# Gathers that skip blank rows: a bound on every indirect load and a row number beyond the table

## The chip, the cores and the metric

The kernel runs on one core of a Trainium2 chip. The metric is the device time of one execution in microseconds (us); the numbers of the kernel before are the median of three runs, and one further execution was recorded by the hardware profiler.

## The reference

Four graph layers are applied in turn to 3125 nodes (64 scalars and 32 three-vectors each, 160 words) over 100000 edges. Cut to what matters here:

```python
edge_index = jnp.stack([src, dst])
h = jnp.maximum(_layernorm(x, axis=-1), 0.0)
x = x + _L0_gnn_ref(h, edge_attr_3, edge_attr_64, ..., edge_index)      # gathers rows dst, sums by src
h = jnp.maximum(_layernorm(x, axis=-1), 0.0)
x = x + _L1_gnn_ref(h, node_vec1, src, dst, edge_attr_4, edge_attr_10, ...)  # gathers src, sums by dst
...
# inside each layer
xs = s[dst]                        # one row of the node table for each edge
tp = ...                           # weights from the edge's own features times that row
agg = jax.ops.segment_sum(tp, src, num_segments=N)
```

Layers 1 to 3 gather the row of `src` and sum by `dst`; `dst` comes sorted. Layers 0, 1 and 3 compute the weights of each edge with a small two-layer network; layer 2 has none.

## The kernel before, in words

The edges are put into tiles of 128 (`P`), so that all edges of a tile fall into one bin of 32 nodes. The number of tiles has to be fixed ahead of the data: 880 (`TILES`), in 110 groups (`GROUPS`) of 8 (`GT`). With the inputs of the reference the bins fill 830 tiles in the order of layer 0 and 832 in that of layers 1 to 3 (counted from `src` and `dst`, 32 nodes to a bin, each bin rounded up to whole tiles); the tiles behind them hold only blank rows. For layer 0 the edge rows are scattered to their slots (`scatter`, L697) over a table that was filled with the blank row `blank[0]`, so the unused slots at the end of each bin's last tile are blank too. For layers 1 to 3 a tile is a copy of 128 consecutive rows of the sorted list (`copy_tiles`), whose start is cut off at 100096 rows, behind which `blank[1]` lies; the last rows of a bin's last tile are then rows of the next bin, with a real index, and only the tiles behind the 832nd are blank.

A blank row has key -1, so that the one-hot matrix that sums the tile has a zero column for it and nothing of it reaches a result. Its index (L641) is a row inside the node table: 3 times the slot's place in its group, between 0 and 3069.

A layer is one pass over the 880 tiles. The work is split by engine, and each engine walks through its own loop of groups with semaphores between them:

- SyncE (SP) loads the edge rows of a group into `rows[q]` (two buffers);
- GpSimd (POOL) issues one indirect DMA a tile (L766), eight a group, that gathers 128 rows of 640 bytes from `table_dram[n]` into `gath[q][:, u, :]`. Ahead of tiles 0 and 4 of a group it waits until the consumer has released that half of the buffer of two groups ago (`prod`, or `sc` in layer 2), ahead of tile 0 also for the edge rows;
- ScalarE (ACT) writes the scaled one-hot matrices `sel` (L900) and the hidden layer (L883);
- TensorE (PE) computes the edge weights (L1559) and the sums of a tile (L1578 in layer 2, L1582 and L1584 in the others);
- VectorE (DVE) multiplies weights and gathered rows (L1245, L1249) and adds the sums to the accumulator `acc` (L1233).

Behind the 880th tile of a layer the sums are transposed and multiplied (L1624, L1632), the next layer's table is made and written, POOL clears `acc` meanwhile (L738), and the next layer's gathers start when the table has landed. Ahead of layer 0 POOL scatters 782 times 128 edge rows (L697); then SP loads the first two groups' rows and DVE clears `acc` (L1179).

`gath` has no other writer than the gathers within a layer; between the layers its space is used for `sumT`.

Of the kernel before, what the change touches and what calls it, by code (L numbers as in the profile page):

```python
# [7 lines left out]
I32 = mybir.dt.int32  # L8
# [12 lines left out]
NPAD = BLOCKS * P  # L21
# [4 lines left out]
GT = 8  # L26
FULL_BINS = PAD_NODE // BIN
MAX_TILES = (EDGES + FULL_BINS * (P - 1)) // P + 1
HALF = GT // 2
# [33 lines left out]
PAD_STEP = NODES // (P * GT)  # L63
# [18 lines left out]
def wait(eng, signal, value):  # L82

    if is_static(value) and value <= 0:
        return
    if isinstance(signal, Signal):
        eng.wait_ge(signal.sem, value + signal.base)
    else:
        eng.wait_ge(signal, value)


def pipeline(eng, n, first, last, extra, body):

    for s in range(first):
        body(s, s // 2, s % 2)
    assert (n - first - last) % 2 == 0
    with eng.Fori(0, (n - first - last) // 2) as i:
        for u in range(first, first + 2):
            body(i * 2 + u, i + u // 2, u % 2)
    for s in range(n - last, n + extra):  # L100
        body(s, s // 2, s % 2)
# [109 lines left out]
def gnn_program(nc, t):  # L211

    ctx = ExitStack()
    with ctx:
        def sb(name, shape, dt=F32):
            return ctx.enter_context(nc.sbuf_tensor(name, shape, dt))

        def sem(name):
            return ctx.enter_context(nc.semaphore(name))
# [41 lines left out]
        gath = [sb(f"gath_{q}", [P, GT, NF]) for q in range(2)]  # L261
# [30 lines left out]
        def carve(words):  # L292
            a = used[0]
            used[0] += words
            assert used[0] <= BINS * 256
            return acc[:, a:a + words]
# [20 lines left out]
        base = [carve(COLS) for _ in range(2)]  # L317
# [13 lines left out]
        blank = [carve(GT * w) for w in (A_W, B_W)]  # L331
# [43 lines left out]
        s_scat = [sem(f"s_scat{q}") for q in range(2)]  # L375
        s_copy = [sem("s_copy_sp"), sem("s_copy_act")]
        s_placed = sem("s_placed")
        s_gp = sem("s_gp")
        s_gd = sem("s_gd")

# [86 lines left out]
        def copy_tiles(eng, kind, part, c):  # L467

            for v in range(0, SPREAD // 2, GT):
                u = part * (SPREAD // 2) + v  # L470
                _, start = nc.values_load_multi_w_load_instructions(
                    starts_row[0:1, bass.ds((c - COPY_FROM) * SPREAD + u, GT)], engines=(kind,),
                    min_val=0, max_val=P * COLS, skip_runtime_bounds_check_because="clamped to the number of edges")
                for w in range(GT):
                    eng.dma_start(tiles_b[:, bass.ds((c - COPY_FROM) * (SPREAD // GT) + u // GT, 1), w, :],
                                  given_dram[bass.ds(start[w], P), :].unsqueeze(1)).then_inc(s_copy[part], 16)
# [155 lines left out]
        def _(pool):  # L632
# [5 lines left out]
                pool.memset(blank[o].rearrange("p (t c) -> p t c", t=GT)[:, :, k:k + 1], -1.0).then_inc(s_blank, 1)  # L638
            for o, k in enumerate((A_IDX, B_IDX)):

                pool.iota(blank[o].rearrange("p (t c) -> p t c", t=GT)[:, :, k].bitcast(I32), pattern=[[PAD_STEP, GT]], base=0,  # L641
                          channel_multiplier=PAD_STEP * GT).then_inc(s_blank, 1)
            pool.memset(ident[:, :], 0.0).then_inc(s_cz, 1)
            pool.memset(tri, 1.0).then_inc(s_cz, 1)
# [13 lines left out]
                               pattern=[[-1, P]], channel_multiplier=1)  # L658

            pool.affine_select(out=tri_h, in_=tri_h, compare_op=ALU.is_gt, fill=0.0, base=0,  # L660
                               pattern=[[1, P]], channel_multiplier=-1)
            pool.affine_select(out=tri, in_=tri, compare_op=ALU.is_gt, fill=0.0, base=0,
                               pattern=[[1, P]], channel_multiplier=-1).then_inc(s_const, 1)
# [66 lines left out]
            for n in range(4):  # L730
                L, S = LAYERS[n], s_e[n]
                if n:

                    clear = -(-BINS * L.width // STORES)
                    for i in range(STORES):
                        a, b = clear * i, min(clear * (i + 1), BINS * L.width)
                        wait(pool, s_c[n - 1]["trn"], -(-b // (4 * LAYERS[n - 1].width)))
                        ins = pool.memset(acc[:, a:b], 0.0)  # L738
                    ins.then_inc(S["zero"].sem, 1)
                if n == 1:  # L740
                    wait(pool, s_c[0]["trn"], BLOCKS)
                    pool.memset(acc[:, tail:], 0.0).then_inc(s_lz, 1)

                if n:
                    wait(pool, s_p[n]["td"], 16 * STORES)
                else:
                    for q in range(2):
                        wait(pool, s_p[n][f"td{q}"], 16 * ((BLOCKS + 1 - q) // 2))
                if n:

                    wait(pool, s_e[n - 1]["sc"], TILES)

                def body(g, half, q, n=n, L=L, S=S):

                    wait(pool, S[f"rows{q}"], (half + 1) * (32 if n == 0 else 16))
                    first, w = (GT * 64 + A_IDX - A_SH, A_W - A_SH) if L.rowsA else (B_IDX, B_W)
                    flat = rows[q][:, :, :].rearrange("p t c -> p (t c)")
                    for u in range(GT):
                        if u % HALF == 0:

                            if L.mlp:
                                wait(pool, S["prod"], g * PAIRS + (u + HALF - 2 * GT) // 2)
                            else:
                                wait(pool, S["sc"], g * GT + (u + HALF - 2 * GT))
                            pool.sem_inc(s_apart["pool"], 1)
                        pool.indirect_dma_start(  # L766
                            gath[q][:, u, :], None, table_dram[n][:, :],
                            bass.IndirectOffsetOnAxis(ap=flat[:, u * w + first:u * w + first + 1].bitcast(I32), axis=0)).then_inc(S[f"ga{q}{u // HALF}"].sem, 16)
                pipeline(pool, GROUPS, 2, 0, 0, body)


# [213 lines left out]
        def _(dve):  # L985
# [182 lines left out]
            for n in range(4):  # L1168
# [86 lines left out]
                def edges(g, half, q, n=n, L=L, o=o, select=select, flush=flush, products=products):  # L1255
                    _, bins = nc.values_load_multi_w_load_instructions(  # L1256
                        tile_bins[0:1, bass.ds(g * GT + (LEAD - 2 * L.lag_fl), GT)], engines=(DVE,), min_val=0, max_val=BINS - 1,
                        skip_runtime_bounds_check_because="counts of at most BINS bins, less one")
                    for u in range(PAIRS):
                        i = g * PAIRS + u  # L1260
                        if within(i - L.lag_fl, TILES // 2):
                            flush(i, u, bins)
                        if L.mlp and within(i, TILES // 2):
                            products(i, u, half, q)
                        if u == 2 and within(g + 1, GROUPS):
                            select(g + 1, half + q, 1 - q)
                        if is_static(g) and g == GROUPS and u == L.lag_fl - 1:
                            break
# [445 lines left out]
```

## Time and profile before

| | |
|---|---|
| median of 3 runs | 6038.6 us (6031.11 to 6040.99) |
| the profiled execution | 6039.14 us, its span 6037.4 us |
| share of the span busy | PE 75%, PEld 65%, DVE 56%, ACT 57%, POOL 70% |
| instructions | 112434 |
| gathers (L766) | 3520, mean 954 ns |
| scatters (L697) | 782, mean 972 ns |

The page's first part gives busy time by engine, its second the span in 40 slices, its third the DMA queues, its fourth the chain of work that ended last, its fifth the costliest groups of instructions with what ended the idle time ahead of them. "issue" is time in which an engine waited for nothing that the profile shows.

### The profile page before, as it was taken

What the parts mean: (1) busy time and instruction counts of PE and PEld (TensorE: products, weight loads), DVE (VectorE), ACT (ScalarE), POOL (GpSimd) and SP (SyncE); (2) the same over time, 40 slices, a digit from 0 to 9 for tenths busy, and PEclk for the clock granted to TensorE, in tenths of its full rate; (3) what the DMA queues carried; (4) which work ended last, traced back from release to release, by engine and by line L of the source; (5) the groups of instructions that cost most, each with busy time, mean ns of one, the idle gap of its engine ahead of it and who ended that gap; (6) DMA issues with size and microseconds to landing.
All of it is one profiled execution on the core that took longest, in us unless ns stands there. A gap on an engine that the chain in (4) does not pass through costs nothing.

```text
span 6037.4 us, 112434 instructions
## 1 busy us (share of the span) xinstructions
PE 4551.9 (75%) x24536; PEld 3911.6 (65%) x24536; DVE 3374.1 (56%) x10505; ACT 3437.0 (57%) x14704; POOL 4216.1 (70%) x4431
## 2 busy tenths in 40 slices
PE   8893122199999998899999985444444788888887
PEld 6552011199988887788888874444444777777776
DVE  8994000288777776566666673222222456666666
ACT  0000000066666665688888866666666577777774
POOL 4757777677777772677777747777777377777773
PEclk7996555599999999999999995555555799999998
DMA  8622333244444441233333323333333123333331
GB/s 283 192 67 72 75 83 79 56 93 93 93 93 93 93 93 26 75 78 78 78 78 78 78 54 79 78 78 78 78 78 78 40 75 78 78 78 78 78 78 45
DMA packets 660123, 507.08 MB, mean 84 GB/s; under 512 B 445302, under 2 KB 563333, under 8 KB 659894
## 3 DMA queue, kind: packets, MB, share of 16 engines
q0 software_dynamic: 195888, 316.94, 21.0%
q1 hardware_dynamic: 381782, 148.41, 10.5%
q10 hardware_dynamic: 82352, 40.52, 2.3%
q8 instruction: 46, 0.75, 0.1%
q14 instruction: 55, 0.45, 0.0%
HBM read 423.69 MB, written 96.48 MB: 86 GB/s over the span
## 4 chain that ended last, share of the span: by engine, by line
POOL 26%; issue 17%; PE 15%; DMA 13%; DVE 5%; DVEq 2%; ACT 1%; SPq 1%; POOLq 1%; ACTq 0%
POOL gath L766 26%; DMA gath<-table,rows 11%; PE bank L1582 3%; PE bank L1559 3%; DMA rows<-rows_a 2%; PE bank L1632 2%; PE bank L1584 2%; DVE work L1249 2%; PE bank L1578 2%; PE bank L1624 1%; DVE acc L1233 1%; PE bank L1535 1%; DVEq L1256 1%; DVE work L1245 1%; ACT sel L900 0%
## 5 line engine op out<-in xcount | busy, mean ns | idle before, releaser
L766 POOL DMA_INDIRECT gath<-table,rows x3520 | 3358.2, 954 | 1160.2 <-issue 1016.2
L900 ACT ACTIVATE sel<-acc,rows 128x32 f32<-128x32 f32 x10560 | 2294.4, 307 | 696.8 <-DVE acc L1224 695.5
L1233 DVE TENSOR_TENSOR acc<-acc,bank 128x160 f32 (+1 forms) x3520 | 1208.3, 343 | 1042.1 <-PE bank L1578 684.7
L1582 PE MATMUL bank<-work,sel 128*128 128x160 f32 (+1 forms) x5280 | 1335.0, 334 | 92.2 <-DVE acc L1233 91.4
L1559 PE MATMUL bank<-w,work 128*128 128x224 f32 (+2 forms) x5280 | 1160.3, 342 | 115.6 <-DVE work L1249 107.2
L1584 PE MATMUL bank<-work,sel 128*128 128x160 f32 x5280 | 1150.4, 300 | 0.0
L1559 PEld LDWEIGHTS bank<-w,work 128*128 128x128 f32 (+1 forms) x5280 | 886.3, 190 | 263.6 <-DVE work L1249 196.7
L1582 PEld LDWEIGHTS bank<-work,sel 128*128 128x128 f32 x5280 | 879.4, 190 | 191.2 <-DVE acc L1233 165.7
L697 POOL DMA_INDIRECT rows_a<-acc x782 | 760.2, 972 | 341.9 <-issue 237.2
L1578 PE MATMUL bank<-gath,sel 128*128 128x160 f32 x1760 | 549.1, 493 | 554.9 <-DMA gath<-table,rows 501.8
L1245 DVE TENSOR_TENSOR work<-bank,gath 128x256 f32<-128x256 f32 x1320 | 556.1, 421 | 719.9 <-DMA gath<-table,rows 707.6
L1584 PEld LDWEIGHTS bank<-work,sel 128*128 128x128 f32 x5280 | 909.8, 190 | 45.7
L1249 DVE TENSOR_TENSOR work<-bank,gath 128x192 f32<-128x192 f32 (+1 forms) x2640 | 896.4, 381 | 0.0
L1578 PEld LDWEIGHTS bank<-gath,sel 128*128 128x128 f32 x1760 | 462.2, 330 | 641.6 <-issue 614.2
L900 ACT ACTIVATE sel<-sel,rows 128x32 f32<-128x32 f32 x2640 | 581.9, 309 | 50.4 <-DVE sel L1224 48.1
L883 ACT ACTIVATE work<-bank 100x512 f32<-100x512 f32 (+1 forms) x440 | 250.9, 596 | 332.8 <-PE bank L1532 225.3
L818 ACT ACTIVATE acc<-acc 128x69 f32 (+1 forms) x34 | 9.3, 273 | 672.9 <-DMA acc<-in_rows_a 557.0
L1460 PE MATMUL bank<-acc,ident 100*128 100x391 f32 (+3 forms) x1000 | 374.5, 475 | 0.0
L1413 PE MATMUL bank<-ident,sel 128*64 128x128 f32 x25 | 10.2, 406 | 452.5 <-ACT sel L801 452.5
L1413 PEld LDWEIGHTS bank<-ident,sel 128*64 128x64 f32 x25 | 4.3, 174 | 455.7 <-issue 455.6
L878 ACT ACTIVATE attrT<-bank 128x256 f32<-128x256 f32 (+1 forms) x330 | 145.3, 440 | 225.4 <-PE bank L1522 206.3
L1122 DVE COPY_PREDICATED acc<-work,bank 128x391 f32<-128x391 int16 (+3 forms) x500 | 253.1, 506 | 34.0 <-PE bank L1460 29.6
(227 smaller groups left out, 3579.1 us busy)
## 6 DMA issues: line engine op xcount, KB each, us to landing
gath<-table,rows POOLq DMA_INDIRECT x3520
rows<-rows_b SPq DMA_DIRECT2D x330, 128.0 KB
rows_a<-acc ACTq DMA_DIRECT2D x1, 30360.0 KB, 101.7
rows<-rows_a SPq DMA_DIRECT2D x110, 256.0 KB
acc<-in_rows_a SPq DMA_DIRECT2D x34, 793.5 KB, 4.8
acc<-in_rows_b SPq DMA_DIRECT2D x34, 368.0 KB, 3.7
rows_given<-acc SPq DMA_DIRECT2D x34, 368.0 KB
rows_a<-acc POOLq DMA_INDIRECT x782
```

The source lines that it names most:

```text
L697: pool.indirect_dma_start(rows_dram[0][:, :], bass.IndirectOffsetOnAxis(ap=pos_r[q][:, u:u + 1], axis=0), stage[0][q][:, u * A_W:(u + 1) * ...
L766: pool.indirect_dma_start(gath[q][:, u, :], None, table_dram[n][:, :], bass.IndirectOffsetOnAxis(ap=flat[:, u * w + first:u * w + first + ...
L900: i = act.activation(sel[q][:, t, at:at + BIN], hot, ACT.Copy, scale=e[:, k:k + 1])
L1122: dve.copy_predicated(pos_f[:, lo:hi], mask, bank(4 + r % PREFIXES, P, 0, hi - lo)).then_inc(s_pick, 1)
L1233: dve.tensor_tensor(sums, sums, bank(6 + b, P, 256 * h, 256 * h + L.width), ALU.add).then_inc(S["fl"].sem, 1)
L1245: dve.tensor_tensor(ps, wt[:, :, 0:128].rearrange("p h (w c) -> p h w c", w=2), two[:, :, 0:S0].unsqueeze(2).to_broadcast([P, 2, 2, S0]), ...
L1249: ins = dve.tensor_tensor(pv, wt[:, h, 128:L.wcols].rearrange("p (w m) -> p w m", w=nv) .unsqueeze(2).to_broadcast([P, nv, 3, V1]), two[:, ...
L1460: pe.matmul(out, ident[0:BINS, b:b + 1].to_broadcast([BINS, P]), base[o][0:BINS, lo:hi], start=False, stop=True).then_inc(s_prefix, 1)
L1559: ins = pe.matmul(bank(4 + u % 2, P, 224 * h, 224 * h + L.wcols), hid, w, start=True, stop=True, skip_group_check=True)
L1578: ins = pe.matmul(out, sel[qv][:, t, 0:128], gath[qv][:, t, :], start=True, stop=True, skip_group_check=True)
L1582: pe.matmul(out, sel[qv][:, t, 96:224], work[:, a + NF:a + NF + L.width], start=True, stop=False, skip_group_check=True)
L1584: ins = pe.matmul(bank(6 + b, P, 256 * h, 256 * h + NF), sel[qv][:, t, 0:128], work[:, a:a + NF], start=False, stop=True, skip_group_check ...
```

## The change

The index of a blank row gets a base of 3200 (`NPAD`), so it lies between 3200 and 6269, behind the table's last row 3199. Every gather carries 3199 as bound, and an index above it is to be skipped without an error, so that nothing is written to its row of `gath`. As such a row would otherwise hold whatever was in the buffer, both gather tiles are cleared once, on POOL, ahead of layer 0, and POOL waits for that. The scatters carry no bound.

```diff
+        s_gz = sem("s_gz")
...
-                pool.iota(blank[o].rearrange("p (t c) -> p t c", t=GT)[:, :, k].bitcast(I32), pattern=[[PAD_STEP, GT]], base=0,
+                pool.iota(blank[o].rearrange("p (t c) -> p t c", t=GT)[:, :, k].bitcast(I32), pattern=[[PAD_STEP, GT]], base=NPAD,
                           channel_multiplier=PAD_STEP * GT).then_inc(s_blank, 1)
...
+                if n == 0:
+                    for q in range(2):
+                        pool.memset(gath[q][:, :, :], 0.0).then_inc(s_gz, 1)
+                    pool.wait_ge(s_gz, 2)
                 if n:
                     wait(pool, s_p[n]["td"], 16 * STORES)
...
                         pool.indirect_dma_start(
                             gath[q][:, u, :], None, table_dram[n][:, :],
-                            bass.IndirectOffsetOnAxis(ap=flat[:, u * w + first:u * w + first + 1].bitcast(I32), axis=0)).then_inc(S[f"ga{q}{u // HALF}"].sem, 16)
+                            bass.IndirectOffsetOnAxis(ap=flat[:, u * w + first:u * w + first + 1].bitcast(I32), axis=0),
+                            bounds_check=NPAD - 1, oob_is_err=False).then_inc(S[f"ga{q}{u // HALF}"].sem, 16)
```

## Rows read from the trace of the kernel before

**Rows 1.** The page: busy time by engine, then POOL and DMA in 40 slices.

```profile
PE 4551.9 (75%) x24536; PEld 3911.6 (65%) x24536; DVE 3374.1 (56%) x10505; ACT 3437.0 (57%) x14704; POOL 4216.1 (70%) x4431
...
POOL 4757777677777772677777747777777377777773
...
DMA  8622333244444441233333323333333123333331
```

**Rows 2.** The page: the costliest groups, gathers and scatters (busy, mean | idle before).

```profile
L766 POOL DMA_INDIRECT gath<-table,rows x3520 | 3358.2, 954 | 1160.2 <-issue 1016.2
...
L697 POOL DMA_INDIRECT rows_a<-acc x782 | 760.2, 972 | 341.9 <-issue 237.2
```

**Rows 3.** Timeline of POOL, end of layer 2: start, duration, instruction, idle before.

```profile
4669.73 0.95 POOL L766 DMA_INDIRECT gath<-table,rows  x1 [0.30 <-issue]
...
4678.53 0.95 POOL L766 DMA_INDIRECT gath<-table,rows  x1 [0.30 <-PE bank L1578]
...
4730.08 0.95 POOL L766 DMA_INDIRECT gath<-table,rows  x1 [0.30 <-issue]
```

**Rows 4.** Timeline of POOL: layer 1's first and last gather, layer 2's first.

```profile
2442.72 0.96 POOL L766 DMA_INDIRECT gath<-table,rows  x1 [43.47 <-issue]
...
3548.62 0.95 POOL L766 DMA_INDIRECT gath<-table,rows  x1 [0.30 <-issue]
...
3624.91 0.96 POOL L766 DMA_INDIRECT gath<-table,rows  x1 [8.40 <-DMA table<-work]
```

**Rows 5.** Waits from 3760 to 4700 us: total, times, longest.

```profile
POOL gath L766 <- PE bank L1578: 8.5, 28, 0.3
```

**Rows 6.** Chain that ended last, ends of layers 1 and 2: start, us, what.

```profile
3548.62 2.58 DMA gath<-table,rows
...
4730.08 2.62 DMA gath<-table,rows
4732.70 0.09 issue
4732.79 2.49 PE bank L1578 x8
```

**Rows 7.** Timeline of POOL, among the scatters: first and last of 20.

```profile
600.17 0.97 POOL L697 DMA_INDIRECT rows_a<-acc  x1 [0.30 <-issue]
...
624.32 0.97 POOL L697 DMA_INDIRECT rows_a<-acc  x1 [0.30 <-issue]
```

**Rows 8.** Groups on POOL: smallest direct transfers, and a clearing of `acc`.

```profile
L674 POOL DMA_DIRECT2D w2v<-in_L_gnn_Wv x3 | 1.5, 504 | 0.0
...
L738 POOL MEMSET acc<- 128x3200 f32 x15 | 41.5, 2766 | 184.8 <-PE bank L1624 184.8
```

**Rows 9.** Timeline of POOL: last scatter, first gathers, sixteenth and seventeenth gather.

```profile
1160.76 0.97 POOL L697 DMA_INDIRECT rows_a<-acc  x1 [0.30 <-issue]
1168.28 1.00 POOL L766 DMA_INDIRECT gath<-table,rows  x1 [6.55 <-DMA rows<-rows_a]
...
1187.19 0.96 POOL L766 DMA_INDIRECT gath<-table,rows  x1 [0.30 <-issue]
1203.76 0.95 POOL L766 DMA_INDIRECT gath<-table,rows  x1 [15.61 <-DMA rows<-rows_a]
```

**Rows 10.** Timeline of DVE at the start of layer 0.

```profile
1169.26 21.39 DVE L1179 MEMSET acc<- 128x25600 f32 x1 [127.62 <-issue]
```

**Rows 11.** Stretches in layers 0 to 3: length, busy of each engine, clock, DMA, GB/s.

```profile
core 0: us, PE busy (x) PEld busy (x) DVE busy (x) ACT busy (x) POOL busy (x), PEclk, DMA share, GB/s
1500.00:1600.00 100.00, 99.82 (x541) 90.28 (x540) 77.87 (x209) 63.04 (x258) 75.92 (x80) 1.00 0.45 93
...
2500.00:2600.00 100.00, 94.84 (x578) 84.27 (x577) 64.25 (x220) 81.81 (x349) 75.92 (x80) 1.00 0.32 79
...
3900.00:4000.00 100.00, 49.51 (x160) 41.60 (x160) 30.00 (x100) 68.32 (x319) 75.61 (x80) 0.50 0.31 78
...
5000.00:5100.00 100.00, 88.85 (x537) 78.42 (x537) 63.65 (x218) 76.92 (x339) 75.78 (x80) 1.00 0.31 78
```

**Rows 12.** The page: GpSimd's DMA queue: packets, MB, share of 16 engines.

```profile
q0 software_dynamic: 195888, 316.94, 21.0%
```

## The prediction

> **What bounds the kernel now.** I read the page's busy shares first: PE shows 75% and POOL 70% [rows 1], which alone would point at PE. The next view, the costliest groups, says more: the first is POOL's gather, 3520 of them at 954 ns, and of the 1160 us that POOL is idle ahead of them 1016 us are "issue", not a wait for another engine [rows 2]. The timeline shows what that is: between 4669.73 and 4730.08 us 49 gathers start, 48 steps in 60.35 us, so one every 1.2573 us: 0.95 busy and 0.30 in between, every time the same [rows 3]. Some of these gaps carry the name of a releaser, and in the waits of layer 2 that entry has 28 cases with a longest of 0.3 us [rows 5]: the buffer was free before POOL asked. So within a layer POOL never waits, and a layer lasts as long as its 880 gathers: layer 1 from 2442.72 to 3548.62, 1105.90 us or 1.2581 a step; layer 2 from 3624.91 to 4730.08, 1105.17 us or 1.2573 a step [rows 3, 4]. The others wait for POOL: the end of a layer is the last gather, 2.6 us until it has landed, and then the consumer [rows 6]. The 16 DMA engines are busy for 0.31 to 0.45 of a stretch [rows 11]. Four passes of 880 gathers are 4425 us of 6039, so the kernel is bound by the rate at which POOL makes descriptors, not by moving the rows.
>
> **What is skipped.** Layer 0 has 112640 slots for 100096 scattered rows: 12544 are blank, and its last 50 tiles are wholly so. Layers 1 to 3 have 48 blank tiles each at the end, 6144 rows. That is 30976 of 450560 rows (6.9%), at 640 bytes 19.8 MB of the queue's 316.94 MB [rows 12]. The number of gather instructions stays 3520.
>
> **Part 1, fewer rows moved.** At a DMA share of 0.31 to 0.45 the moved bytes hide under POOL's issuing, so taking away 6.9% is worth nothing in the stream. It shows only where a landing is waited for: behind the last gather of a layer, which is blank in all four. It takes 2.62 us from start to landing, of which 0.95 is POOL's own [rows 3, 6]; the other 1.67 us is data and completion together. No row shows a transfer that moves nothing, so the saving lies between 0 and 1.67 us, four times, 0 to 6.7 us. I take 0.5 us each, 2 us in all, nearer to nothing because the completion signal must still come.
>
> **Part 2, the bound on every gather.** This decides. No row shows an indirect transfer with a bound, so it is bounded from both sides. Two things could be added: work for POOL's sequencer ahead of the instruction (the bound has to be in a register) and work in making the descriptors (128 indices are compared, some left out). For the first a row exists: ahead of tiles 0 and 4 of each group the sequencer has a wait and a semaphore step more than ahead of the others, and the gap is 0.30 us there too [rows 3]. So instructions of that kind run while the gather before is still busy, and cost nothing. For the second, the low end is nothing, if the same loop compares anyway. The high end is a test row by row: a direct transfer of 32 rows takes 504 ns and a gather of 128 takes 954 [rows 2, 8], so another 96 rows (and the indirection) cost 450 ns, 4.7 ns a row; a compare that costs a sixth of a row's whole work is 0.8 ns a row, 100 ns a gather. Between them is the one place where the trace shows two variants of this same instruction: scatters take 24.15 us for 19 steps, 1.2711 us each, against 1.2573 for gathers [rows 3, 7], 13.8 ns more. A variant of the indirection is thus worth some ten nanoseconds, and the bound is nearest to that. I take 13.8 ns.
>
> It is paid where POOL sets the pace: in layers 1 to 3 on 2640 gathers; in layer 0 on all but the first 16, because the seventeenth waits 15.61 us for its edge rows anyway, behind the 21.39 us in which DVE clears the accumulator [rows 9, 10]. 864 + 2640 = 3504 gathers by 13.8 ns are 48.4 us. Nothing covers it: in a layer's stream each nanosecond a gather is 3.5 us of the total.
>
> The Trainium skill, page "DMA: Bandwidth & Descriptors", section "Anatomy of one DMA", calls descriptor generation small and variable and says that many descriptors can be emitted before the incremental cost shows. The trace doesn't agree for this instruction: 954 of every 1257 ns are POOL's. By that page neither the compare nor the skipped rows would show, and the sum would be Part 1 alone. The page "Perfetto Trace Analysis", section on the software-generated DMA instruction, says that its end in a profile is when the last processor has written its descriptors, and advises start-to-start spacing for this engine; spacing is what the sums here use, and by durations alone (972 less 954) the term would be 63 us.
>
> **Part 3, clearing the gather tiles.** Two memsets of 128x1280 words on POOL: 2766 ns for 3200 words [rows 8] is 0.864 ns a word, so 1.1 us each, 2.3 with the wait. They stand between the last scatter (ends 1161.73) and the first gather (1168.28), where POOL waits 6.55 us, last for the edge rows [rows 9]. Should some of it stick out, the 15.61 us stall ahead of the seventeenth gather takes it up. Cost nothing; without either cover it would be 2.3 us. What is queued behind the new wait is only the first gather, and DVE's start isn't behind it, since POOL's signal that lets DVE clear the accumulator comes earlier. The new base of the index fill costs nothing: same instruction, other constant.
>
> **The sum.** 6039.1 (the profiled execution, 0.5 us above the median) + 48.4 - 2 = 6085.5; I say 6085. What is late next is the same thing, POOL.
>
> **Rivals.** (a) *The bound costs nothing and skipping saves nothing on POOL.* For it: the constant 0.30 gap, and code that compares in any case. Against: some work is added to a loop whose every nanosecond shows. Time 6039.1 less 0 to 6.7, about 6037; it covers added costs up to 3.4 ns a gather.
>
> (b) *Faster: a blank gather is cheap for POOL.* If leaving out all 128 rows brings a gather down to that of the smallest direct transfer, 504 + 304 ns, its step falls from 1.257 to 0.81 us, and the others set the pace over the last 48 or 50 tiles of a layer, 60 us. In layer 0 PE is busy 99.8% (nothing to gain), in layer 1 94.8% (3 us), in layer 3 88.9% (7 us), in layer 2 the greatest is ACT's 68.3%, so 19 us [rows 11]. With landings 35 us at most, 6004; with half of it 6020. It decides if a wholly blank gather saves over 10% of its step and the bound costs under 3 ns. Against: the index reads, the 16 completions and the fixed part remain.
>
> (c) *Slower by much: the test is made row by row, in the loop that writes descriptors.* 100 ns by 3504 is 350 us, 6390; at the double 6740. For it: 450 ns for 96 rows looks like a loop over rows. Against: nothing in the trace shows how many rows are handled at once.
>
> (d) *The bound doesn't take the blank rows out.* Then the queue's bytes stay at 316.94 MB and only Part 2's cost is left, 6087.
>
> **How the numbers follow.** A measurement here can tell about 0.2% from no change, 12 us, which is 3.4 ns a gather. My forecast, a bound that costs 3.4 to 30 ns, with (d): 0.36 (6050 to 6142). (c), over 30 ns: 0.19. (a): 0.27. (b): 0.18, centred on 6015. Slower 0.55, same 0.27, faster 0.18. The range from 6008 to 6400 leaves out the extreme of (b), some 4%, and the worse part of (c), some 11%. As cases of both signs hold the chance, the likeliest one's own range is 6050 to 6142.
>
> **What would show it.** Right: 49 gathers at the end of layer 2 with a step of about 1.271 us, mean duration about 968 ns, the 0.30 gap unchanged, 3520 of them; queue bytes near 297.1 MB; layer 1's stream 1118 us instead of 1106; seventeenth gather at about 1204 as now; memsets ended before 1168. If the gap grows instead of the duration, the cost is in the sequencer. If blank gathers, the last 48 of layer 2, are shorter than the rest of that layer, (b) is at work; if longer, leaving a row out is a costly branch, and I have the sign of that term wrong. The prediction is wrong if the step is the same to 3 ns, or above 1.36 us.

## The result and the profile after

The changed kernel takes 6230.9 us (median of 4, 6228.45 to 6233.33) against 6036.1 for the kernel before: ratio 1.0323, 95% interval 1.0305 to 1.0341, slower by 195 us. The profiled execution took 6230.53 us, 191.4 more than the one of before. Eight of the sixteen experiments below ran on two other chips, on which the kernel before itself takes 8333 us, for a reason that stays open; they are marked "8333-us chip", and where nothing else is said only the durations of single instructions are used of them, which agree with those of the other chips within 4 ns.

The page of the changed kernel: busy time, DMA by slices, the queue that POOL fills, gathers and scatters. They answer to [rows 1, 2, 12].

```profile
PE 4569.7 (73%) x24536; PEld 3912.5 (63%) x24536; DVE 3368.3 (54%) x10505; ACT 3440.8 (55%) x14704; POOL 4417.5 (71%) x4433
...
DMA  8623233244444430222222212222222022222220
...
q0 software_dynamic: 195888, 297.18, 18.9%
...
L771 POOL DMA_INDIRECT gath<-table,rows x3520 | 3555.8, 1010 | 1154.7 <-issue 1029.9
...
L698 POOL DMA_INDIRECT rows_a<-acc x782 | 761.4, 974 | 338.0 <-issue 237.2
```

The queue's bytes are gone as counted (316.94 to 297.18 MB), with the same 195888 packets. (The page's own line for HBM traffic says 423.69 MB read for both kernels, and for every kernel below that only skips rows; it doesn't show the skipping.) The number of gathers is the same; each takes 1010 ns in place of 954. The scatters, which carry no bound, are as before. No other engine is busier by more than 18 us.

What one gather looks like, from its line in the changed kernel (min/median/max in ns, first and last start); the median of before was 953:

```profile
L771 POOLq MOVE  x3520: 29/29/38, 1164.9 to 6125.3; - x196
L771 POOL DMA_INDIRECT gath<-table,rows x3520: 1002/1006/1251, 1165.7 to 6137.6; - x196
```

The timeline of POOL after the change: layer 1's first and last gather, layer 2's first, one of its blank stretch (the last 48) and its last. They answer to [rows 3, 4].

```profile
2500.58 1.01 POOL L771 DMA_INDIRECT gath<-table,rows  x1 [43.55 <-DMA table<-work]
...
3652.43 1.00 POOL L771 DMA_INDIRECT gath<-table,rows  x1 [0.30 <-issue]
...
3727.25 1.01 POOL L771 DMA_INDIRECT gath<-table,rows  x1 [8.46 <-DMA table<-work]
...
4868.56 1.01 POOL L771 DMA_INDIRECT gath<-table,rows  x1 [0.30 <-issue]
...
4879.05 1.01 POOL L771 DMA_INDIRECT gath<-table,rows  x1 [0.30 <-issue]
```

Layer 1: (3652.43 - 2500.58) / 879 = 1.3104 us a step, against 1.2581. Layer 2: (4879.05 - 3727.25) / 879 = 1.3104, against 1.2573. The gap within a layer is still 0.30: the whole 53 ns is in the duration. The last eight steps of layer 2, over wholly blank tiles, are (4879.05 - 4868.56) / 8 = 1.311 us: a gather that moves nothing costs POOL exactly what any other costs.

The start of layer 0, on POOL and with the clearing, answers to [rows 9]:

```profile
1158.27 0.97 POOL L698 DMA_INDIRECT rows_a<-acc  x1 [0.30 <-issue]
1161.47 2.27 POOL L747 MEMSET gath<- 128x1280 f32 x2 [2.24 <-issue]
1165.75 1.07 POOL L771 DMA_INDIRECT gath<-table,rows  x1 [2.00 <-issue]
...
1201.54 1.00 POOL L771 DMA_INDIRECT gath<-table,rows  x1 [15.04 <-DMA rows<-rows_a]
```

From the last scatter's start to the first gather's it is 7.48 us, before 7.52; the seventeenth gather still stalls for 15 us. The clearing took 2.27 us and cost nothing.

The loss splits by layer. Gathers in a stretch of layer 0 (1250 to 2250 us), before the change and after it, then of layer 2 (3760 to 4600 us) after it:

```profile
L766 POOL DMA_INDIRECT gath<-table,rows x792 | 758.7, 958 | 241.4 <-issue 224.3 <-DMA rows<-rows_a 16.5 <-DVE work L1249 0.6
```

```profile
L771 POOL DMA_INDIRECT gath<-table,rows x752 | 771.4, 1026 | 229.1 <-issue 224.8 <-DMA rows<-rows_a 4.3
```

```profile
L771 POOL DMA_INDIRECT gath<-table,rows x642 | 645.5, 1005 | 195.6 <-issue 185.2 <-DMA rows<-rows_b 7.3 <-PE bank L1584 3.0
```

2640 gathers of layers 1 to 3 by 52.8 ns a step are 139 us. In layer 0 the median goes from 953 to 1006 ns too, 46 us for 864 gathers; its mean goes up by 68 ns in this stretch, because a few gathers that take up to 1.25 us are more numerous in this execution (90 of the layer's 880 against 19). Kernels without a bound have as many (see the part on why the prediction was right or wrong); over the whole layer they add 12 us. Less 1.9 us of earlier landings (below) and 2.2 us by which layer 0's stream started earlier, that is 193 of 191.4 us.

### The profile page after: what moved, and what is told of

Same layout as the page of the kernel before. It is cut to its first block, busy times and chain, and to the rows that moved or that the text cites. A ratio compares the mean times of both kernels' runs of the same rounds, so it can differ in the third digit from the quotient of the medians.

```text
span 6228.9 us, 115956 instructions
## 1 busy us (share of the span) xinstructions
PE 4569.7 (73%) x24536; PEld 3912.5 (63%) x24536; DVE 3368.3 (54%) x10505; ACT 3440.8 (55%) x14704; POOL 4417.5 (71%) x4433
## 3 DMA queue, kind: packets, MB, share of 16 engines
q0 software_dynamic: 195888, 297.18, 18.9%
HBM read 423.69 MB, written 96.48 MB: 84 GB/s over the span
## 4 chain that ended last, share of the span: by engine, by line
issue 33%; POOL 29%; DMA 8%; PE 7%; POOLq 2%; DVE 1%; SPq 1%; ACT 1%; DVEq 0%; ACTq 0%
POOL gath L771 29%; DMA gath<-table,rows 5%; DMA rows<-rows_b 3%; PE bank L1638 2%; PE bank L1630 1%; POOLq L771 1%; PE bank L1584 1%; PE bank L1588 0%; DMA rows<-rows_a 0%; POOLq L97 0%; PE bank L1565 0%; DVE acc L1185 0%; SPq L615 0%; PE bank L1590 0%; POOLq L87 0%
## 5 line engine op out<-in xcount | busy, mean ns | idle before, releaser
L771 POOL DMA_INDIRECT gath<-table,rows x3520 | 3555.8, 1010 | 1154.7 <-issue 1029.9
```

Source lines behind the costliest of these rows:

```text
L771: pool.indirect_dma_start(gath[q][:, u, :], None, table_dram[n][:, :], bass.IndirectOffsetOnAxis(ap=flat[:, u * w + first:u * w + first + ...
```

## The experiments

Each kernel is given by its edit.

**The bound alone.** Rivals: the bound costs, or leaving rows out costs.

```diff
 # kernel before
-   ... .bitcast(I32), axis=0)).then_inc(...)
+   ... .bitcast(I32), axis=0),
+       bounds_check=NPAD - 1, oob_is_err=False).then_inc(...)
```

> The kernel before with the bound alone, on another chip than its first run, so that POOL sets the pace again. Theory A (the bound costs whatever is skipped): step 1.31 us, total 6036 + about 190 = 6226 to 6233, within 0.1% of the changed kernel. Were a third of the loss due to skipped rows or to the clearing, it would be near 6165.

Measured: 6231.3 us, ratio 1.0307 (1.0291 to 1.0322); the interval overlaps that of the changed kernel's 1.0323. The kernel before takes 6045.8 us on this chip, so the loss is 185.5 us, and 3504 gathers by 52.8 ns are 185.0. Its gathers on the page:

```profile
L766 POOL DMA_INDIRECT gath<-table,rows x3520 | 3553.6, 1010 | 1158.6 <-issue 988.4
```

Nothing is skipped here, 316.94 MB are moved, and the loss is there, but for 9 us that lie within the intervals. The other parts of the change, skipped rows and clearing, add or save nothing that can be measured. The same kernel had run first on an 8333-us chip:

> The kernel before with the bound 3199 on every gather and nothing else: blank rows still name rows inside the table, no tile is cleared, nothing is skipped. Theory A (the bound itself is what costs, in making the descriptors): step of a gather 1.31 us as in the changed kernel, mean duration about 1.01 us, gap 0.30; total 6036 + 3504 x 0.0533 = about 6223 to 6233, up to 2 us above the changed kernel since the last landing of each layer is not shortened. Theory B (leaving rows out is what costs, by a slower path taken once any row of the run is beyond the bound): step 1.257 us, total 6036. Theory C (both): between.

There it took 8305.6 against 8333.3 us, ratio 0.9962 (0.9937 to 0.9988), although its gathers took a median of 1009 ns, 52 more than the 957 of a kernel without the bound on that chip (the clearing alone, below). Its gathers on the page:

```profile
L766 POOL DMA_INDIRECT gath<-table,rows x3520 | 3553.8, 1010 | 2758.1 <-issue 1031.2
```

POOL is idle for 2758 us ahead of its gathers there, against 1159 in the run above; the gaps of 0.30 us are in both, so some 1600 us are waits for others. That is the control: a longer gather shows in the time only where POOL sets the pace. That it is paid out of the waits is argued from these two numbers; why this run is even 28 us faster than the kernel before stays open.

**The move of the bound into a register.** A MOVE of 29 ns stands ahead of each gather. Rivals: the cost is in the gather itself, or partly in that move.

```diff
 # changed kernel
+            bound = pool.alloc_register("gather_bound")
+            pool.reg_mov(bound, NPAD - 1)
             for n in range(4):
...
-                            bounds_check=NPAD - 1, oob_is_err=False)
+                            bounds_check=bound, oob_is_err=False)
```

> The changed kernel, but the bound is moved into a register once ahead of the four layers, in place of a move ahead of each of the 3520 gathers. Theory A (cost in making the descriptors): step stays 1.31 us, total 6231. Theory D (the move ahead of each gather, 29 ns in the trace, is part of the cost): step 1.28 us, 29 ns less by 3504 is 102 us, total about 6130.

Measured (8333-us chip, so the total says nothing): the 3519 other moves are gone, 112437 instructions in place of 115956, and the gather's median stays 1006 ns. The next run but one confirms it on a chip where POOL sets the pace: with 0 as bound no move is issued at all, and the median is 1006 too. The move hides under the gather before it, as the semaphore steps do.

**More rows skipped.** What would a skipped row cost or save?

```diff
 # changed kernel
-                            bounds_check=NPAD - 1, oob_is_err=False)
+                            bounds_check=NPAD // 2 - 1, oob_is_err=False)
```

> The changed kernel with 1599 as bound, so that 49% of the real rows in layers 1 to 3 and 28% in layer 0 are skipped too, mixed among kept rows in nearly every gather; what those edges would add is left out of the result. Theory A (one price for a gather with a bound, whatever is skipped): step 1.31 us, total 6229 to 6231, queue bytes about 170 MB. Theory of a branch for each skipped row: with b ns for one such row, 45 to 60 skipped rows a gather make the step longer by about 50 b ns; already 1 ns would give 1.36 us and 6400. Theory of cheaper skipped rows: step below 1.31 us.

Measured: 6239.4 us in one execution, 8 us over the 6229 to 6231 expected, median of a gather 1006 ns, queue bytes 180.08 MB (expected about 170). Nearly half of the rows left out, mixed among kept ones, doesn't move the median: there is no branch by row to pay, and nothing to win. The mean step of layers 1 and 3 is 1.320 and 1.322 us in place of 1.310, by 41 and 49 gathers of over 1.15 us in them, which are taken up behind the experiments.

```diff
-                            bounds_check=NPAD - 1, oob_is_err=False)
+                            bounds_check=0, oob_is_err=False)
```

> The changed kernel with 0 as bound: nearly all rows are skipped (the messages of the edges are left out of the result). Theory A: POOL's step stays 1.31 us although next to nothing is moved, total 6225 to 6231 (landing shorter, and every consumer waits for POOL as before). If moving rows had any part in the pace, the step falls.

Measured: 6211.9 us in one execution, 19 less than the changed kernel and 13 under the range expected. The queue and the gathers, from its page and its groups:

```profile
q0 software_dynamic: 195888, 31.55, 3.3%
...
L771 POOL DMA_INDIRECT gath<-table,rows x3520 | 3545.5, 1007 | 1154.3 <-issue 1040.6 <-DMA table<-work 66.7 <-PE bank L1584 22.8
```

285 MB less are moved than before the change, and the kernel is still 181 us slower than the kernel before on the same chip. The packets are the same 195888. A gather of 128 rows has 48 of them ((195888 - 186672) / 192, with the 104 groups below), one of 64 or of 32 rows has 32, and one whose rows are all skipped still 48: to skip rows is not the same as to ask for fewer. That each skipped row keeps an entry, which would explain why POOL saves nothing, is argued and not shown, since one packet stands for several rows. Of the 19 us, 15 are in layer 0, whose mean gather is 1006 ns in place of 1024; its stream started 5 us earlier, and 5 us are given back in layer 2, where 56 gathers are long.

**Does the price go by row?** Gathers of fewer partitions, without and with the bound; both clear the tiles once.

```diff
 # kernel before, and kernel before with the bound
-   gath[q][:, u, :], ...  ap=flat[:, ...]
+   gath[q][0:64, u, :], ...  ap=flat[0:64, ...]      # and 0:32
```

> The kernel before plus the clearing of the gather tiles, but each gather fetches the rows of partitions 0 to 63 alone (the messages of the other half are left out of the result). It gives the price of rows on POOL. If the 450 ns between a direct transfer of 32 rows and a gather of 128 are a price by row of 4.7 ns, the duration falls from 953 by about 300 ns to 650 and the step to 0.95 us; below about 1.06 us a step other engines set the pace in part of the layers.

> The same with the bound 3199 on every gather. If the bound costs by row: half of the 53 ns more than the run with 64 rows and no bound, 27 ns. If it is a fixed price of an instruction: the full 53 ns more in duration.

> The kernel before plus the clearing, each gather fetching the rows of partitions 0 to 31 alone (the messages of the other edges are left out of the result). From 953 ns at 128 rows and 905 at 64, a straight line of 0.75 ns a row gives a duration of 881 ns. If rows are handled in batches, or the fixed part shrinks otherwise, it will be off that line by more than 5 ns.

> The same with the bound 3199 on every gather. The bound added 53 ns at 128 rows and 38 at 64: a straight line gives 23 ns fixed and 0.23 ns a row, so 31 ns here, a duration of 912 ns. If the price is all fixed apart from noise: about 38 ns as at 64 rows.

Median duration of a gather in ns:

| rows | without bound | with bound | difference |
|---|---|---|---|
| 128 | 953 | 1006 | 53 |
| 64 | 905 | 943 | 38 |
| 128 (8333-us chips) | 957 | 1009 | 52 |
| 32 (8333-us chip) | 860 | 904 | 44 |

The totals with 64 rows are 5888.7 and 6004.3 us. The expectation for the bare gather was far off: 650 ns expected at 64 rows, 905 measured. Between 64 and 128 rows a row costs (953 - 905) / 64 = 0.75 ns, not 4.7. The straight line from there gave 881 ns at 32 rows; 860 were measured, (957 - 860) / 96 = 1.0 ns a row on the 8333-us chips. By an estimate from these numbers some 830 ns are paid for any gather at all. The bound's 38 ns at 64 rows lie between the two expectations (27 by row, 53 fixed), and the straight line for it (31 ns at 32 rows, 912 in all) was missed with 44 and 904. So its price is mainly fixed too, about 40 ns, with 10 to 15 more between 64 and 128 rows; it isn't a line through three sizes, and 4 ns between chips are of the size of what is left, so a finer split stays open.

**The error mode.**

```diff
 # kernel before with the bound
-       bounds_check=NPAD - 1, oob_is_err=False)
+       bounds_check=NPAD - 1, oob_is_err=True)
```

> As the run with the bound alone, but an index beyond the bound is to be reported as an error; no index is beyond it. If the price is the compare: step 1.31 us again. If it is the silent skipping mode that selects a slower path: step 1.257 us, total 6036.

> The bound with the error mode, nothing beyond it, on a chip where POOL sets the pace. Its first run showed a median duration of 1022 ns against 1009 and 1006 with the silent mode. If the error mode has a price of its own of 13 to 16 ns: step 1.325 us, total 6231 + 3504 x 0.015 = 6284. If that was the other chip: 6231.

Measured on the two 8333-us chips: a median of 1022 ns both times, against 1009 (bound alone) and 1006 (bound in a register) in silent mode on the first of them. So the error mode costs 13 to 16 ns more, though nothing is beyond the bound, and the silent mode isn't what makes a gather slow. What it does to the total where POOL sets the pace wasn't seen.

**A bound on the scatters.** Is it a price of every indirect transfer?

```diff
 # kernel before, L697
-                        stage[0][q][:, u * A_W:(u + 1) * A_W], None).then_inc(s_scat[q], 16)
+                        stage[0][q][:, u * A_W:(u + 1) * A_W], None,
+                        bounds_check=SLOTS - 1, oob_is_err=False).then_inc(s_scat[q], 16)
```

> The kernel before with a bound (last slot, nothing beyond it) on the 782 scatters instead of on the gathers. If the price belongs to indirect transfers of either direction: the scatter's duration rises from 0.967 by about 53 ns to 1.02 us; POOL waits for ACT ahead of some scatters only, so about 782 x 0.053 = 41 us more, 6077. If the bound is checked on the read side alone: no change, 6036.

Measured: 6039.6 us, no difference, and the scatter's line shows the move and the same duration (967 ns before, too):

```profile
L697 POOLq MOVE  x782: 29/29/29, 126.4 to 1135.1; - x196
L697 POOL DMA_INDIRECT rows_a<-acc x782: 966/967/1301, 127.3 to 1150.6; - x196
```

The step is (624.78 - 599.31) / 20 = 1.2735 us in this kernel's timeline, against 1.2711 of [rows 7]. Of the two expectations the one of 53 ns fell: a bound on the scatters costs 2 ns at most. Why the two sides differ stays open. It agrees with the move being free.

**The clearing alone.**

> The kernel before plus the two memsets of the gather tiles and the wait for them. All theories: they lie between the last scatter and the first edge rows and in front of a stall of 15 us, so 6036 within 0.1%. Were they on the path, 2.3 us more.

> The kernel before plus the two memsets of the gather tiles and the wait, on a chip where POOL sets the pace. All theories: no change, ratio 1.000 within its interval. On the path it would be 2.3 us, 0.04%, which the ratio can't show but the start of the seventeenth gather can: it should not be later than in the kernel before by 2 us against the last scatter.

```diff
 # kernel before
+        s_gz = sem("s_gz")
...
+                if n == 0:
+                    for q in range(2):
+                        pool.memset(gath[q][:, :, :], 0.0).then_inc(s_gz, 1)
+                    pool.wait_ge(s_gz, 2)
```

Both on 8333-us chips: ratios 0.9993 (0.9970 to 1.0016) and 1.0012 (0.9987 to 1.0037). Too blunt for 2 us. The start of layer 0 in the changed kernel, above, shows the first cover at work; that of the first of these two runs shows it failing and the second cover taking over:

```profile
1647.76 2.27 POOL L747 MEMSET gath<- 128x1280 f32 x2 [16.77 <-issue]
1650.98 1.01 POOL L771 DMA_INDIRECT gath<-table,rows  x1 [0.95 <-POOL gath L747]
```

Here the memsets start late and the first gather waits for them: it comes 20.95 us after the last scatter's start, against 18.59 in the run with the error mode on the same chip, which clears nothing. The seventeenth gather comes 57.85 us after it, against 57.66: the 2.4 us are gone in the stall.

**What do the blank tiles cost?** 104 groups in place of 110, which these inputs fit; not for any others.

```diff
 # kernel before
-GROUPS = -(-MAX_TILES // GT)
+GROUPS = 104
```

> The kernel before with 104 groups in place of 110, which these inputs just fit (830 and 832 tiles): the 48 blank tiles of each layer are not computed by any engine. It is exact for these inputs alone. If the blank tiles cost what their gather instructions cost, 4 x 48 x 1.2573 = 241 us less: 5795. If they cost less because other work fills their time, more than that remains.

Measured: 5805.7 us, ratio 0.9603 (0.9588 to 0.9618), 240 us less where 241 were expected. A blank tile that no engine works on saves its gather's step of 1.257 us, and that is what there is to win; its bytes are worth nothing.

**Leave out the instruction, not the rows.** No bound; POOL looks up the bins of a group and branches for each half group.

```diff
 # kernel before, ahead of each layer's gathers, then their body
+                pool.wait_ge(s_tbs[1 if n else 0], 16)
...
+                    _, bins = nc.values_load_multi_w_load_instructions(
+                        tile_bins[0:1, bass.ds(g * GT + LEAD, GT)], engines=(POOL,), ...)
+                    for half_u in (0, HALF):
+                        ...                             # the waits as before
+                        with pool.If(bins[half_u] != BINS - 1):
+                            for u in range(half_u, half_u + HALF):
+                                pool.indirect_dma_start(...)        # as before
+                        with pool.Else():
+                            pool.dma_start(gath[q][0:16, half_u, :], table_dram[n][0:16, :]).then_inc(S[f"ga{q}{half_u // HALF}"].sem, 16 * HALF)
```

> The kernel before without any bound, but POOL reads the bins of a group's tiles into registers and branches: where the first of four tiles lies behind the last bin, the four gathers are left out and one small direct transfer of 16 rows raises the semaphore instead. That takes away the instructions that cost, not the rows. From the busy shares of the others over the last 48 tiles (PE 94.8% in layer 1, ACT 68% in layer 2, PE 89% in layer 3): 3 + 19 + 7 = 29 us less at most, 6007, if loads and branches hide under the running gather as the semaphore steps do. If each group's load and branch shows with 0.1 us, 44 us more: about 6050.

Measured: 6009.5 us against 6045.8 of the kernel before on the same chip, ratio 0.9936 (0.9923 to 0.9950), 36 us less (30 to 47 by the interval) where 29 were expected at most from the busy shares. The shares gave the size and not the places: against the trace with a bound on the scatters, on the same chip, layer 1 is 6 us shorter (3 expected), layer 2 is 15 (19) and layer 3 is 14 (7), and layer 0 is 5 longer. It beats both kernels. The end of layer 2, where the gathers stop and small transfers stand in their place:

```profile
4675.92 0.96 POOL L770 DMA_INDIRECT gath<-table,rows  x1 [0.30 <-issue]
4676.88 1.06 POOL L774 DMA_DIRECT2D gath<-table  x2
4684.48 0.49 POOL L774 DMA_DIRECT2D gath<-table  x1 [6.54 <-PE bank L1584]
4685.26 0.49 POOL L774 DMA_DIRECT2D gath<-table  x1 [0.28 <-PE bank L1584]
```

Gaps of 6.54 us, released by PE: POOL waits for others for the first time in this layer's stream. In front of them the gap of a gather is still 0.30, and the step of layers 1 to 3 is 1.260 us against 1.2575 in that same trace: loading eight registers and branching twice a group hides but for some 2 ns a gather, 8 us in all. The chain from 4675 to 4712 us says who is late next:

```profile
by line: ACT sel L906 59.7%; PE bank L1584 18.6%; DMA gath<-table,rows 9.0%; issue 5.0%; DVE acc L1239 2.9%; POOL gath L770 2.6%; DVE acc L1230 1.2%; DVEq L1239 0.6%; DVE small L1220 0.5%; DVEq L87 0.5%; DVEq L1220 0.2%; ACTq L97 0.2%; ACTq
```

ACT's one-hot matrices, 60% of that stretch, as the shares of [rows 11] had it for layer 2. The remaining 200 of the 240 us are, by difference, the other engines' own work on blank tiles.

## Why the prediction was right or wrong

- *What bounds the kernel*: right. POOL's step in the stream sets the time, each nanosecond a gather is 3.5 us; the control on the 8333-us chip shows the reverse.
- *What is skipped*: right, 19.76 MB gone where 19.8 were counted.
- *Part 1, fewer rows*: right in place and size. The chain behind the last gather of layer 2 now reads as below, against 2.62 of [rows 6]: 0.47 us less from its start, where I took 0.5. In the kernel with the bound alone it is 2.54, so 0.39 to 0.47 is the worth of the missing rows. That 0.5 was near is luck in part: it was picked between 0 and 1.67.

```profile
4879.05 2.15 DMA gath<-table,rows
```

- *Part 2, the bound*: this step failed, in its size. The mechanism was the forecast one: in the duration and not in the gap, on every gather, 3504 of them on the path, the register for nothing. But the term was taken as 13.8 ns (48.4 us) and measures 53, 185 us over 3504 gathers. The step of 1.310 us lies between the forecast 1.271 and the 1.36 that the prediction named as its sign of being wrong. The choice was wrong, "nearest to the one place where two variants of the instruction differ": the difference between scatter and gather says nothing about a compare, and the scatter run shows that a bound on that very variant costs 2 ns at most. With an upper end of 100 ns and no row near, the middle would have been 50 ns and a total of 6212; that would have been near by luck, since the upper end was badly founded too. The low end was favoured without a reason.
- *The upper bound* rested on 4.7 ns a row, from a direct transfer of 32 rows and a gather of 128. That compared two instructions, not two sizes: the row's price is 0.75 to 1.0 ns. That 53 ns lay under the 100 is luck, by the sixth that was taken of it.
- *Part 3, the clearing*: right; each of the two covers hid it in one of the traces.
- *The long gathers of layer 0*: not foreseen. In the changed kernel 90 of its 880 take 1.05 to 1.25 us, nearly always the third of a group:

```profile
1714.16 1.25 POOL L771 DMA_INDIRECT gath<-table,rows  x1 [0.30 <-issue]
...
1724.89 1.21 POOL L771 DMA_INDIRECT gath<-table,rows  x1 [0.30 <-issue]
```

Both stand at the moment when SP issues the second load of edge rows (1714.15 and 1725.00 us) and DVE makes its one-hots. But neither the bound nor the traffic of the gathers is needed for them. The first line is from layer 0 of the kernel before, the second from layer 2 with all rows skipped:

```profile
1468.17 1.20 POOL L766 DMA_INDIRECT gath<-table,rows  x1 [0.30 <-issue]
```

```profile
3998.38 1.25 POOL L771 DMA_INDIRECT gath<-table,rows  x1 [0.30 <-PE bank L1584]
```

Counting those more than 4% over their layer's median, the kernel before has 19 of them in layer 0, and without a bound on the gathers on another chip 66 (bound on the scatters), 52 (104 groups) and 73 (branches); with it 104 (bound alone), 82 (half skipped) and 5 (all skipped). All of these but the first and the last two ran on one chip, and there they lift the mean of layer 0 over its median by 15 ns with the bound on the gathers and by 13 to 17 ns in the three kernels without it; the means with the bound on the scatters and on the gathers, 969 and 1021 ns, are again 52 apart. In the kernel before, 91 more gathers meet both the load and the one-hots and aren't long; the 41 and 49 in layers 1 and 3 with half of the rows skipped and the 56 in layer 2 with all skipped meet neither. So what makes them long stays open, and how many there are differs from one execution to the next: they are 12 us of this loss, because the profiled execution of before had few, and nothing makes them a part of the bound's price.
- *Rivals*: (a), (b) and (d) fell: blank gathers are neither cheaper nor dearer, and the rows are skipped. Of (c) the place was right (the gather's own duration) and so was the size, since it began above 30 ns and had 0.19; its mechanism was not: the price is mainly fixed and not by row. The page "DMA: Bandwidth & Descriptors" of the Trainium skill, section "Anatomy of one DMA", calls descriptor generation small and says that many descriptors can be emitted before the incremental cost shows. The first half disagrees with the 953 ns here, of which some 830 are fixed. The second is nearer to the runs than the prediction took it: 64 more rows add 48 ns. What the prediction worked out from the page, no cost for the bound, was wrong by 53 ns a gather.
- *The range*, 6008 to 6400, held the time; the direction was right; the likeliest case's own range (6050 to 6142) didn't hold it.

## What to carry to other kernels

If GpSimd's gathers follow each other with a constant gap, the kernel pays for gather instructions, not for rows or bytes: a bound that skips rows saves nothing there and costs 53 ns for each gather of 128 rows. Save whole instructions instead; register loads and a branch ahead of them hid here but for some 2 ns a gather, and the next engine's busy share gave roughly how much could be won (29 us against 36). When an operation isn't in the trace and the ends are far apart, don't slide to the end that a look-alike row is near to; ask first whether that row has the cost in question in it.

## What the runs showed of the hardware that was not expected

- A gather costs POOL 860, 905 and 953 ns at 32, 64 and 128 rows, plus the 0.30 us gap: nearly all of it is fixed.
- A bound adds 44, 38 and 53 ns at those sizes on a gather, 2 ns at most on a scatter of 128 rows; the error mode adds 13 to 16 ns to that.
- With all rows skipped the packet count stays at 195888 while the queue's bytes fall to 31.55 MB, of which 28.58 are not the gathers' (316.94 less 3520 x 128 x 640 bytes). A wholly blank gather lands 2.15 us after its start in place of 2.54 to 2.62.
- Some gathers take up to 0.25 us more than the rest, with and without a bound, with and without rows to move, in numbers that differ between executions (in layer 0 from 5 to 104 of 880). The cause is open.
